# A Flamingo block on one Trainium2 core: the key weights' high parts shared between ScalarE and VectorE on the way to the loop

## The chip, the cores and the metric

The kernel is one program on one core of a Trainium2 chip. The metric is the time of one execution on the device, in microseconds (us), and less is better. The engines are TensorE (PE; PEld is its weight load), VectorE (DVE), ScalarE (ACT), GpSimd (POOL) and SyncE (SP), which issues the loads and stores. Each engine works through its own queue in order, and semaphores tie the queues together.

## What is computed

Eight batches of 224 tokens attend to 750 context rows and to themselves, with a gated residual, and then go through a gated feed-forward layer of spiking neurons. The part that matters here is the layer norm of the inputs and the keys and values made of them:

```python
def layernorm(x, g, b):
    mu = jnp.mean(x, axis=-1, keepdims=True)
    var = jnp.var(x, axis=-1, keepdims=True)
    return (x - mu) * jax.lax.rsqrt(var + EPS) * g + b
xn = layernorm(x, gm, bm)              # x: the 750 context rows of a batch, 512 wide
ln = layernorm(latents, gl, bl)        # latents: its 224 tokens, normalised once before
q = ln @ Wq
kv = jnp.concatenate([xn, ln], axis=-2) @ Wkv
k, v = jnp.split(kv, 2, axis=-1)
q, k, v = (heads(q), heads(k), heads(v))
q = q / scale
sim = jnp.einsum('bhid,bhjd->bhij', q, k)
attn = jax.nn.softmax(sim - stop_gradient(max(sim)), axis=-1)
out = jnp.einsum('bhij,bhjd->bhid', attn, v)
x = x + jnp.tanh(g_xattn[0]) * (out @ Wout)
# then h = square(relu(layernorm(x) @ W_fc.T)), y = h @ W_proj.T, five threshold steps, x + tanh(g_ffn) * spikes / 5
```

## The kernel before

**Numbers in two parts.** Every product with a weight is made of two-part numbers: a high part in the format fp32r (part 0) and the rest, value minus high part (part 1). A product is three passes: high by high, rest of the weight by high, high by rest of the data. For a weight `w` of 512 x 512 there are four pieces (k = 0 to 3, 128 rows each). `split_hi` (ACT, L1339) writes a piece's high part from the staged load, and `split_lo` writes its rest: on DVE at L1801, on POOL at L2099. `w_hi` counts the high parts, `w_lo[i]` the rests of weight i, where i is 0 for the keys (`wk`), 1 for the queries (`wq`), 2 for the values (`wv`), 3 for the output (`wo`).

**Tiles.** The 974 rows of a batch (750 of context, 224 tokens) lie in eight tiles: 0 to 3 of 128 rows, 4 and 5 of 119, 6 and 7 of 112. For the first batch, DVE makes mean and variance of two tiles at a time (`first_statistics`, L1593 to L1604), POOL the scale factors (`first_root_of`, L2036 and L2088). The scaling of tiles 0, 2, 5, 7 is on ACT (`first_norm`, L1349), that of 1, 3, 4, 6 on POOL (L2093). PE transposes the scaled tiles (`first_transposes`, L813): tiles 0 to 3 give the first 512 columns, tiles 4 to 7 the other 462. ACT writes the high part of each of four transposed chunks into `xT` (`hi_chunks`, L1142), DVE the rest (`lo_chunks`, L1614). Two columns at each end of `xT` hold offset vectors; ACT (L1365) and DVE (L1820) write them.

**The way to the loop.** Ahead of the loop over the batches, all queues are written out by hand, in one fixed order each. PE's is: six warming transposes, tiles 0 to 3, the first key products (`first_keys_hi`), tiles 4 to 7, the passes with the rest of `xT` (`first_keys_lo`), the second keys, queries, first scores, first values. `first_keys_hi` takes piece k as soon as its high part and chunk k are there, then waits for all four rests (`w_lo[0]`) and does the passes with them. The four transposes of tile 4 overwrite the bank from which the rest of chunk k is read, so each waits for that rest (`xlo_done`).

SP loads in this order: tiles 0 and 1, tiles 2 and 3, the key weights in two halves (`wk_in[0]` for pieces 0 and 1, `wk_in[1]` for 2 and 3), tiles 4 and 5, tiles 6 and 7, the query weights, and, once the key rests are there, the value weights.

On DVE, behind the statistics of tiles 0 to 3, stand the rests of pieces 0 and 1, the end columns, one small difference (`dshift`, L1821), the statistics of tiles 4 to 7, then the rests of the four chunks. On POOL, behind tiles 1 and 3, stand the rests of pieces 2 and 3, then the factors and the scaling of tiles 4 and 6.

Of the kernel before, what the change touches and what calls it, by code (L numbers as in the profile page):

```python
# [20 lines left out]
def flamingo_block(nc, x, ctx_in, g_xattn, g_ffn, Wq, Wkv, Wout, gm, bm, gl, bl, WfcT, WprojT, out):  # L21
# [5 lines left out]
    DC = D // P  # L27
# [43 lines left out]
    with keep:  # L71
        def sb(stack, name, shape, dt=F32):
            return stack.enter_context(nc.sbuf_tensor(name, shape, dt))

        def sem(name):
            return keep.enter_context(nc.semaphore(name))
# [33 lines left out]
        wk = sb(a, "wk", [P, 2, DC, D], F32R)  # L110
# [91 lines left out]
        def kq_index(c, u, first):  # L202

            return FIRST.index((c, u)) if first else 3 * c + u
# [9 lines left out]
        def kq_bank(c, u, first):  # L214
# [2 lines left out]
                return (work[0], work[1], heads_out, work[0], work[1], heads_out, maxes, work[1])[FIRST.index((c, u))]  # L217
            return work[kq_index(c, u, first) % 2]

        def value_bank(t):  # L220
            return work[(t + t // VF) % 2]

# [21 lines left out]
        gate_half = sem("gate_half")  # L244
        w_in = [sem(f"w_in{i}") for i in range(4)]
        w_hi = sem("w_hi")
        w_lo = [sem(f"w_lo{i}") for i in range(4)]
        wk_in = [sem(f"wk_in{i}") for i in range(2)]
        pair_in = [sem(f"pair_in{i}") for i in range(TILES // 2)]
# [104 lines left out]
        staged = [vals[:, (i % 2) * DC:(i % 2 + 1) * DC, :] for i in range(4)]  # L354
# [140 lines left out]
        def _(pe):  # L495
# [53 lines left out]
            def values(b, t, after_out=False, first=False):  # L549

                if t < 2:
                    pe.wait_ge(kq_done, (4, 8)[t] if first else b * 12 + (7 + t))
                elif t < 6:
                    if after_out:
                        pe.wait_ge(x1_done[t - 4], b + 1)
                    pe.wait_ge(v_done, b * VF + (t - 1))
                elif t == 6:
                    pe.wait_ge(v_done, b * VF + 6)
                else:
                    pe.wait_ge(kq_done, b * 12 + 9)  # L560
                product(value_bank(t)[0:ROWS[t], :], lambda i, k: xT[:, i, k, XO + AT[t]:XO + AT[t] + ROWS[t]],
                        lambda i, k: wv[:, i, k, :], DC).then_inc(v_mm, 1)
# [260 lines left out]
            def first_product(c, w, a, k, u=0, start=False, stop=False):  # L823

                lo, hi = ((0, HALF), (XO + half_of(c, True), XO + KEYS))[u]
                return pe.matmul(kq_bank(c, u, True)[:, 0:hi - lo], wk[:, w, k, c * P:(c + 1) * P], xT[:, a, k, lo:hi],  # L826
                                 start=start, stop=stop)

            def first_keys_hi():

                pe.wait_ge(ends_hi, 2)
                for k in range(DC):
                    pe.wait_ge(w_hi, k + 1)
                    pe.wait_ge(xhi_done, k + 1)
                    for c in range(2):
                        first_product(c, 0, 0, k, start=(k == 0))
                pe.wait_ge(w_lo[0], DC)
                for c in range(2):
                    for k in range(DC):
                        first_product(c, 1, 0, k)  # L840
                for w in range(2):
                    for k in range(DC):
                        first_product(2, w, 0, k, start=(w == 0 and k == 0))
# [32 lines left out]
            warm(6)  # L876
            first_transposes(0, 1, 2, 3)
            first_keys_hi()
            first_transposes(4, 5, 6, 7)
            first_keys_lo()  # L880
# [176 lines left out]
        def _(act):  # L1057
# [76 lines left out]
            def hi_chunks(b, g, *ks):  # L1134

                for k in ks:
                    if g == 0 and k == 0:
                        act.wait_ge(kq_mm, b * 12)
                        act.wait_ge(v_mm, b * TILES)
                    act.wait_ge(tr_done, b * 2 * DC + (g * DC + k + 1))  # L1140
                    if g == 0:
                        act.activation(xT[:, 0, k, XO:XO + HALF], score[:, k, 0:HALF], ACT.Copy,  # L1142
                                       scale=gain[:, 0, k:k + 1]).then_inc(xhi_done, 1)
                    else:
                        act.activation(xT[:, 0, k, XO + HALF:XO + T], score[:, k, 0:2 * CT], ACT.Copy,
                                       scale=gain[:, 0, k:k + 1])
                        act.activation(xT[:, 0, k, XO + T:XO + KEYS], score[:, k, 2 * CT:2 * CT + L], ACT.Copy,
                                       scale=gain[:, 2, k:k + 1]).then_inc(xhi_done, 1)
# [184 lines left out]
            def split_hi(i, w, *ks):  # L1333
                for k in ks:
                    if i == 0:
                        act.wait_ge(wk_in[k // 2], 16)
                    else:
                        act.wait_ge(w_in[i], 16)
                    act.activation(w[:, 0, k, :], staged[i][:, k, :], ACT.Copy,  # L1339
                                   scale=QSCALE if i == 1 else 1.0).then_inc(w_hi, 1)  # L1340
# [5 lines left out]
            def first_norm(t):  # L1346
                r = ROWS[t]
                act.wait_ge(first_rstd, t // 2 + 1)
                act.activation(xin[0:r, t, :], xin[0:r, t, :], ACT.Identity, bias=nmr[0:r, t:t + 1],  # L1349
                               scale=rstd[0:r, t:t + 1]).then_inc(ln_act, 1)  # L1350
# [5 lines left out]
            act.wait_ge(const_ready, 4)  # L1356
            act.activation(gate[:, 0:1], halfneg[:, 0:1], ACT.Copy)
            first_norm(0)
            split_hi(0, wk, 0, 1)
            act.wait_ge(vec_mm, 1)  # L1360
            act.activation(gain[:, :, :], heads_out[:, 0:4 * DC].rearrange("p (v k) -> p v k", v=4),
                           ACT.Copy).then_inc(gain_ready, 1)
            act.wait_ge(gain_ready, 1)
            for end in ENDS:
                act.activation(xT[:, 0, :, end], end_columns, ACT.Copy).then_inc(ends_hi, 1)  # L1365
            act.activation(offsets[:, 0, :, LT:P], bm_columns, ACT.Copy).then_inc(shift_hi, 1)
            first_norm(2)
            split_hi(0, wk, 2, 3)
            hi_chunks(0, 0, 0, 1, 2, 3)
            first_norm(5)  # L1370
            first_norm(7)
            split_hi(1, wq, 0, 1, 2)
# [95 lines left out]
        def _(dve):  # L1468
# [117 lines left out]
            def first_statistics(i):  # L1586

                ts = (2 * i, 2 * i + 1)
                dve.wait_ge(pair_in[i], 16)
                if i == 2:  # L1590
                    dve.wait_ge(ends_in, 16)
                for t in ts:
                    dve.bn_stats(bn[0:ROWS[t], t, :], xin[0:ROWS[t], t, :]).then_inc(bn_done, 1)  # L1593
                dve.wait_ge(bn_done, ts[-1] + 1)
                dve.tensor_copy(tick[:, 0:1], halfneg[:, 0:1])
                for t in ts:
                    dve.bn_aggr(mv[0:ROWS[t], t, :], bn[0:ROWS[t], t, :]).then_inc(mv_done, 1)
                two = slice(2 * i, 2 * i + 2)
                dve.wait_ge(mv_done, ts[-1] + 1)
                dve.tensor_scalar(nmu[:, two], mv[:, two, 0], -1.0, None, ALU.mult)  # L1600
                if i < 3:
                    dve.tensor_scalar(ve[:, two], mv[:, two, 1], EPS, None, ALU.add).then_inc(first_ve, 1)
                else:
                    dve.tensor_scalar(ve[:, two], mv[:, two, 1], 1.0 + EPS, EPS * EPS, ALU.mult,  # L1604
                                      ALU.add).then_inc(first_ve, 1)
# [191 lines left out]

            def split_lo(i, w, *ks):
                for k in ks:
                    dve.wait_ge(w_hi, i * DC + (k + 1))  # L1800
                    dve.scalar_tensor_tensor(w[:, 1, k, :], staged[i][:, k, :], QSCALE if i == 1 else 1.0,  # L1801
                                             w[:, 0, k, :].bitcast(F32), ALU.mult, ALU.subtract).then_inc(w_lo[i], 1)

# [9 lines left out]
                dve.tensor_copy(tick[:, 1 + i:2 + i], halfneg[:, 0:1]).then_inc(x1_done[i], 1)  # L1813
            first_statistics(0)
            first_statistics(1)
            split_lo(0, wk, 0, 1)
            dve.wait_ge(gain_ready, 1)
            for i, end in enumerate(ENDS):
                dve.wait_ge(ends_hi, i + 1)
                dve.tensor_tensor(xT[:, 1, :, end], end_columns, xT[:, 0, :, end].bitcast(F32), ALU.subtract)  # L1820
            dve.tensor_tensor(dshift[:, :], gain[:, 3, :], gain[:, 1, :], ALU.subtract).then_inc(dshift_done, 1)  # L1821
            first_statistics(2)
            first_statistics(3)
            lo_chunks(0, 0)
# [195 lines left out]
        def _(pool):  # L2020
# [69 lines left out]
            def first_norm(t):  # L2090
                r = ROWS[t]
                pool.wait_ge(first_rstd, t // 2 + 1)
                pool.tensor_scalar(xin[0:r, t, :], xin[0:r, t, :], rstd[0:r, t:t + 1], nmr[0:r, t:t + 1],  # L2093
                                   ALU.mult, ALU.add).then_inc(ln_pool, 1)

            def split_lo(i, w, *ks):
                for k in ks:
                    pool.wait_ge(w_hi, i * DC + (k + 1))
                    pool.tensor_tensor(w[:, 1, k, :], staged[i][:, k, :], w[:, 0, k, :].bitcast(F32),  # L2099
                                       ALU.subtract).then_inc(w_lo[i], 1)  # L2100

# [51 lines left out]
```

## Time and profile before

| | us |
|---|---|
| median of 3 runs | 1043.2 |
| lowest and highest of them | 1042.61, 1043.29 |
| the profiled execution | 1042.75 |
| its span, first to last instruction | 1040.9 |
| PE busy | 1024.1 (98% of the span) |
| DVE busy | 781.9 (75%) |
| ACT busy | 592.0 (57%) |
| POOL busy | 311.2 (30%) |

The span is what the trace shows; the time of an execution is a little longer, since it holds what lies around the first and the last instruction. Busy shares are means over the whole program. The stretch that the change touches is the first 20 us or so, and it is read from timelines of that stretch.

### The profile page before, as it was taken

To read this page: it belongs to the slowest core of one execution; us is meant where nothing else is said; L and a number is where in the kernel's file an instruction comes from. 1 tells how busy PE (TensorE), PEld (TensorE's weight loads), DVE (VectorE), ACT (ScalarE), POOL (GpSimd) and SP (SyncE) were. 2 spreads that over 40 slices of the span, in tenths; PEclk is the share of its full clock that TensorE was granted. 3 is DMA by queue.
4 is the path that set the end of the run, shared out by engine and by line. 5 is a ranking of instruction groups with operands and counts; after the bars stand their busy time and mean duration, and the time that the engine had idled before them with its cause. 6 is when DMAs were issued, how large, how long until landed. Compare 5 with 4: busy or idle time off the path is not lost.

```text
span 1040.9 us, 18764 instructions
## 1 busy us (share of the span) xinstructions
PE 1024.1 (98%) x6919; PEld 840.9 (81%) x6919; DVE 781.9 (75%) x1228; ACT 592.0 (57%) x1147; POOL 311.2 (30%) x289
## 2 busy tenths in 40 slices
PE   6999999999999999999999999999999999999997
PEld 5878778878878877887887887777888888998887
DVE  7589978887896897888789687879433654584766
ACT  6667476566457647656645764566455433455535
POOL 5444443444336344344433634343000000000000
PEclk9999999999999999999999999999999999999999
DMA  6402001100300400110030020132430001201011
GB/s 199 136 2 78 2 1 56 58 1 10 102 0 0 112 0 0 60 52 0 10 102 0 0 76 0 36 94 60 149 122 21 1 1 41 82 1 41 21 61 42
DMA packets 32232, 47.54 MB, mean 46 GB/s; under 512 B 2617, under 2 KB 11849, under 8 KB 32185
## 3 DMA queue, kind: packets, MB, share of 16 engines
q1 hardware_dynamic: 32132, 46.87, 14.5%
q8 instruction: 30, 0.49, 0.2%
q14 instruction: 17, 0.14, 0.0%
q10 hardware_dynamic: 53, 0.04, 0.0%
HBM read 39.56 MB, written 7.34 MB: 45 GB/s over the span
## 4 chain that ended last, share of the span: by engine, by line
PE 94%; DVE 4%; DMA 1%; issue 1%; ACT 0%; SPq 0%; DVEq 0%
PE work L501 40%; PE work L660 14%; PE score L673 13%; PE heads_out L610 9%; PE score L584 9%; PE score L516 2%; PE heads_out L622 1%; PE score L929 1%; PE work L826 1%; DVE top L1479 1%; DMA vals<-in_L_xattn_Wkv 1%; DVE on L1563 1%; PE maxes L597 1%; DVE probs L1515 1%; PE heads_out L501 0%
## 5 line engine op out<-in xcount | busy, mean ns | idle before, releaser
L2031 POOL TENSOR_TENSOR dsum<-dsum,probs 128x448 f32<-128x448 f32 (+1 forms) x186 | 219.9, 1182 | 14.6
L501 PE MATMUL work<-wv,xT 128*128 128x512 f32 (+2 forms) x768 | 187.1, 398 | 0.4 <-DVE kst L1528 0.4
L501 PE MATMUL work<-xT,wk 128*128 128x512 f32 (+2 forms) x708 | 167.5, 388 | 0.0
L501 PEld LDWEIGHTS work<-wv,xT 128*128 128x128 f32 (+2 forms) x768 | 137.6, 183 | 37.0 <-issue 2.3
L660 PE MATMUL work<-zT,wf 128*128 128x512 f32 (+1 forms) x768 | 164.1, 364 | 0.0
L1067 ACT ACTIVATE probs<-score 128x448 f32<-128x448 f32 (+2 forms) x256 | 119.2, 548 | 76.9 <-PE score L584 76.9
L660 PEld LDWEIGHTS work<-zT,wf 128*128 128x128 f32 x768 | 131.5, 189 | 23.0 <-issue 0.7
L501 PEld LDWEIGHTS work<-xT,wk 128*128 128x128 f32 x708 | 129.7, 188 | 24.4 <-DVE qst L1533 0.4
L1515 DVE TENSOR_TENSOR probs<-probs,maxes 128x1792 f32<-128x1792 f32 x64 | 128.4, 2017 | 1.1
L2028 POOL TENSOR_TENSOR dsum<-probs 128x448 f32<-128x448 f32 x31 | 35.7, 1150 | 277.9 <-ACT probs L1073 277.9
L673 PE MATMUL score<-hT,wp 128*128 128x512 f32 (+1 forms) x576 | 117.4, 354 | 0.0
L2036 POOL TENSOR_TENSOR rstd<-ve,halfneg 128x4 f32<-128x4 f32 (+1 forms) x22 | 25.0, 1134 | 284.9 <-ACT ve L1173 200.7
L673 PEld LDWEIGHTS score<-hT,wp 128*128 128x128 f32 x576 | 96.1, 189 | 14.9
L1190 ACT ACTIVATE relu<-work 128x512 f32<-128x512 f32 (+1 forms) x64 | 34.8, 543 | 123.5 <-PE work L660 123.3
L584 PEld LDWEIGHTS score<-qst,kst 64*128 64x128 f32 (+2 forms) x1536 | 87.6, 181 | 21.2 <-issue 21.0
L610 PE MATMUL heads_out<-probs,vals 128*64 128x224 f32 (+1 forms) x992 | 100.8, 356 | 0.0
L1072 ACT ACTIVATE probs<-probs 128x1344 f32<-128x1344 f32 x64 | 85.7, 1338 | 26.4 <-DVE probs L1515 26.4
L584 PE MATMUL score<-qst,kst 64*128 64x224 f32 (+2 forms) x1536 | 99.8, 275 | 0.0
L1654 DVE TENSOR_TENSOR hT<-h,hT 128x512 fp32r<-128x512 f32 (+1 forms) x48 | 29.1, 606 | 87.9 <-ACT hT L1202 87.6
L610 PEld LDWEIGHTS heads_out<-probs,vals 128*64 128x64 f32 (+1 forms) x992 | 68.4, 137 | 26.6 <-issue 5.6
L1479 DVE TENSOR_TENSOR top<-score,top 112x448 f32<-112x448 f32 (+1 forms) x128 | 72.1, 617 | 17.7 <-ACT probs L1067 17.4
L1528 DVE SCALAR_TENSOR_TENSOR kst<-work,shift,kst 128x224 fp32r<-128x224 f32 (+4 forms) x93 | 48.6, 551 | 25.7 <-ACT kst L1099 13.8
(218 smaller groups left out, 1428.0 us busy)
## 6 DMA issues: line engine op xcount, KB each, us to landing
xin<-in_ctx SPq DMA_DIRECT2D x28, 256.0 KB, 3.9
neuron<-in_L_ffn_W_fc SPq DMA_DIRECT2D x16, 256.0 KB, 3.1
neuron<-in_L_ffn_W_proj SPq DMA_DIRECT2D x16, 256.0 KB, 2.9
xin<-in_ctx SPq DMA_DIRECT2D x14, 238.0 KB
xin<-in_x SPq DMA_DIRECT2D x14, 224.0 KB, 7.0
zt<-x_scratch SPq DMA_DIRECT2D x3, 1024.0 KB, 5.7
fin<-x_scratch SPq DMA_DIRECT2D x3, 1024.0 KB, 5.6
out<-fin SPq DMA_DIRECT2D x10, 256.0 KB, 2.1
```

Of the source, the lines that this page charges most:

```text
L501: mm = pe.matmul(bank, lhs(i, k), rhs(j, k), start=(n == 0), stop=(n == len(passes) * chunks - 1))
L584: mm = pe.matmul(score[0:ROWS[t], 2 * (k % 2) + e, t % 2 * L:(t % 2 + 1) * L], kst[rows, s, i, AT[t]:AT[t] + ROWS[t]], qst[rows, s, j, :], ...
L610: mm = pe.matmul(bank[e * DH:(e + 1) * DH, 0:L], vals[0:ROWS[t], t, h * DH:(h + 1) * DH], probs[0:ROWS[t], h % 4, t * L:(t + 1) * L], star ...
L660: mm = pe.matmul(up_bank(j)[:, 0:n], wf[:, w, j, k * P:(k + 1) * P], zT[:, a_, k, 0:n], start=(m == 0 and k == 0), stop=(m == len(PASSES) ...
L673: mm = pe.matmul(score[:, d, 0:n], wp[:, w, j, d * P:(d + 1) * P], h_part(g, j, a_)[:, 0:n], start=(j == 0 and m == 0), stop=(j == FC - 1 ...
L1067: act.activation(probs[0:r, (2 * p + e) % 4, 2 * k * L:(2 * k + 2) * L], score[0:r, 2 * (k % 2) + e, 0:2 * L], ACT.Copy).then_inc(s_copied, 1)
L1072: act.activation(probs[:, h % 4, 0:CTX_TILES * L], probs[:, h % 4, 0:CTX_TILES * L], ACT.Exp)
L1479: dve.tensor_tensor(top[0:r, e, :], score[0:r, 2 * (k % 2) + e, 0:2 * L], other, ALU.max).then_inc(top_done, 1)
L1515: dve.tensor_tensor(v, v, row.to_broadcast([P, TILES, L]), ALU.subtract).then_inc(sub_done, 1)
L1528: ins = dve.scalar_tensor_tensor(kst[:, s, 1, lo:hi], bank[:, lo - at:hi - at], shift[:, 0, c, v:v + 1], kst[:, s, 0, lo:hi].bitcast(F32), ...
L2028: pool.tensor_tensor(total, tile(0), tile(1), ALU.add).then_inc(dchain, 1)
L2031: pool.tensor_tensor(total[0:ROWS[t]], total[0:ROWS[t]], tile(t), ALU.add).then_inc(dchain if t < TILES - 1 else dsum_done, 1)
```

## The change

The high parts of key pieces 2 and 3 are now made by DVE, by a plain copy from the staged load (L1825 in the new numbering), ahead of the end columns; the rests of pieces 0 and 1 move behind `dshift`. A new semaphore, `wk_hi_late`, counts these two copies, and `hi_ready` gives the semaphore and the count for a piece's high part. On ACT, tile 2 is scaled behind piece 0, piece 1 comes behind the end columns, and the offsets' small write comes behind the four chunks. POOL still makes the rests of pieces 2 and 3, and waits for the copies.

```diff
+        def hi_ready(i, k):
+            if i == 0:
+                return (w_hi, k + 1) if k < 2 else (wk_hi_late, k - 1)
+            return w_hi, 2 + (i - 1) * DC + (k + 1)
...
                 for k in range(DC):                      # PE, first_keys_hi
-                    pe.wait_ge(w_hi, k + 1)
+                    pe.wait_ge(*hi_ready(0, k))
                     pe.wait_ge(xhi_done, k + 1)
...
             first_norm(0)                                # ACT
-            split_hi(0, wk, 0, 1)
+            split_hi(0, wk, 0)
+            first_norm(2)
             act.wait_ge(vec_mm, 1)
...
             for end in ENDS:
                 act.activation(xT[:, 0, :, end], end_columns, ACT.Copy).then_inc(ends_hi, 1)
+            split_hi(0, wk, 1)
+            hi_chunks(0, 0, 0, 1, 2, 3)
             act.activation(offsets[:, 0, :, LT:P], bm_columns, ACT.Copy).then_inc(shift_hi, 1)
-            first_norm(2)
-            split_hi(0, wk, 2, 3)
-            hi_chunks(0, 0, 0, 1, 2, 3)
             first_norm(5)
...
             first_statistics(1)                          # DVE
-            split_lo(0, wk, 0, 1)
+            for k in range(2, DC):
+                dve.wait_ge(wk_in[1], 16)
+                dve.tensor_copy(wk[:, 0, k, :], staged[0][:, k, :]).then_inc(wk_hi_late, 1)
             dve.wait_ge(gain_ready, 1)
...
             dve.tensor_tensor(dshift[:, :], gain[:, 3, :], gain[:, 1, :], ALU.subtract).then_inc(dshift_done, 1)
+            split_lo(0, wk, 0, 1)
             first_statistics(2)
...
             def split_lo(i, w, *ks):                     # DVE and POOL
                 for k in ks:
-                    pool.wait_ge(w_hi, i * DC + (k + 1))
+                    pool.wait_ge(*hi_ready(i, k))
```

How the queues stand, first ACT's at the start: `xin` is a tile (L1349, L1356 in the new numbering: the scaling), `wk` a weight piece, `gain` the layer norm vectors, `xT` of 4x2 an end column pair, `xT` of 512 a chunk. Before:

```order
L1349 ACTIVATE xin<-xin,nmr,rstd 128x512
L1339 ACTIVATE wk<-vals 128x512 x2
L1361 ACTIVATE gain<-heads_out 128x16
L1365 ACTIVATE xT<-gain 128x4x2 x2
L1366 ACTIVATE offsets<-gain 128x4x16
L1349 ACTIVATE xin<-xin,nmr,rstd 128x512
L1339 ACTIVATE wk<-vals 128x512 x2
L1142 ACTIVATE xT<-score,gain 128x512 x4
```

ACT's queue at the same place now:

```order
L1356 ACTIVATE xin<-xin,nmr,rstd 128x512
L1346 ACTIVATE wk<-vals 128x512
L1356 ACTIVATE xin<-xin,nmr,rstd 128x512
L1369 ACTIVATE gain<-heads_out 128x16
L1373 ACTIVATE xT<-gain 128x4x2 x2
L1346 ACTIVATE wk<-vals 128x512
L1149 ACTIVATE xT<-score,gain 128x512 x4
L1376 ACTIVATE offsets<-gain 128x4x16
```

The second tile has moved up by six operations, two pieces have left the queue, and the offsets come behind the chunks. DVE's queue from the end of the statistics of tiles 2 and 3 to those of tiles 4 and 5 (`BN_STATS`), before:

```order
L1602 TENSOR_SCALAR ve<-mv 128x2
L1801 SCALAR_TENSOR_TENSOR wk<-vals,wk 128x512 x2
L1820 TENSOR_TENSOR xT<-gain,xT 128x4x2 x2
L1821 TENSOR_TENSOR dshift<-gain 128x4
L1593 BN_STATS bn<-xin 119x6 x2
```

DVE's queue at the same place now:

```order
L1609 TENSOR_SCALAR ve<-mv 128x2
L1825 CAST wk<-vals 128x512 x2
L1829 TENSOR_TENSOR xT<-gain,xT 128x4x2 x2
L1830 TENSOR_TENSOR dshift<-gain 128x4
L1808 SCALAR_TENSOR_TENSOR wk<-vals,wk 128x512 x2
L1600 BN_STATS bn<-xin 119x6 x2
```

Two copies have come in ahead of the end columns, and the two rests stand between `dshift` and the next statistics. The rows of POOL and PE are the same as before, but for what they wait for.

## Rows read from the trace of the kernel before

**Rows 1.** The page: the span, and PE's busy time.

```profile
span 1040.9 us, 18764 instructions
...
PE 1024.1 (98%) x6919; PEld 840.9 (81%) x6919; DVE 781.9 (75%) x1228; ACT 592.0 (57%) x1147; POOL 311.2 (30%) x289
```

**Rows 2.** Chain of waits, 0 to 50 us: start us, us, what.

```profile
1.74 7.09 DMA vals<-in_L_xattn_Wkv
...
13.04 4.28 PE work L826 x16
...
36.32 0.99 ACT probs L1067 x2
```

**Rows 3.** Timeline, ACT: start us, us, engine, line, operation, count, [idle before <-releaser].

```profile
8.85 1.15 ACT L1339 ACTIVATE wk<-vals 128x512 fp32r<-128x512 f32 x2 [0.55 <-DMA vals<-in_L_xattn_Wkv]
...
10.10 0.31 ACT L1365 ACTIVATE xT<-gain 128x8 fp32r<-128x8 f32 x2
...
10.46 0.80 ACT L1349 ACTIVATE xin<-xin,nmr,rstd 128x512 f32<-128x512 f32 x1
...
11.17 1.14 ACT L1339 ACTIVATE wk<-vals 128x512 fp32r<-128x512 f32 x2
...
12.21 2.42 ACT L1142 ACTIVATE xT<-score,gain 128x512 fp32r<-128x512 f32 x4
```

**Rows 4.** Timeline, PE: transposes L813, products L826 (15.31 is the ninth).

```profile
9.18 1.78 PE L813 MATMUL score<-ident,xin 128*128 128x128 f32 x8
...
11.32 1.10 PE L813 MATMUL score<-ident,xin 128*128 128x128 f32 x8 [0.35 <-ACT xin L1349]
13.04 4.28 PE L826 MATMUL work<-xT,wk 128*128 128x512 f32 x16 [0.63 <-ACT xT L1142]
...
15.31 0.40 PE L826 MATMUL work<-xT,wk 128*128 128x512 f32 x1
...
18.98 1.75 PE L813 MATMUL score<-ident,xin 119*128 119x119 f32 x16
```

**Rows 5.** Timeline, DVE; last, line L1820 alone: ns min/median/max, first and last start.

```profile
7.84 0.51 DVE L1600 TENSOR_SCALAR nmu<-mv 128x2 f32<-128x2 f32 x1
...
9.52 1.29 DVE L1801 SCALAR_TENSOR_TENSOR wk<-vals,wk 128x512 fp32r<-128x512 f32 x2 [1.11 <-ACT wk L1339]
...
10.73 0.66 DVE L1820 TENSOR_TENSOR xT<-gain,xT 128x8 fp32r<-128x8 f32 x2
...
12.49 1.29 DVE L1593 BATCH_NORM_STATS2 bn<-xin 119x6 f32<-119x512 f32 x2 [1.03 <-DMA xin<-in_ctx]
...
16.19 2.72 DVE L1614 SCALAR_TENSOR_TENSOR xT<-score,gain,xT 128x512 fp32r<-128x512 f32 x4
...
L1820 DVE TENSOR_TENSOR xT<-gain,xT x2: 159/369/579, 10.7 to 10.8; 128x8 fp32r<-128x8 f32 x2
```

**Rows 6.** Timeline, POOL: scaling L2093, rests L2099.

```profile
7.55 0.77 POOL L2093 TENSOR_SCALAR xin<-xin,rstd,nmr 128x512 f32<-128x512 f32 x1
...
9.57 1.80 POOL L2093 TENSOR_SCALAR xin<-xin,rstd,nmr 128x512 f32<-128x512 f32 x1
...
11.87 2.52 POOL L2099 TENSOR_TENSOR wk<-vals,wk 128x512 fp32r<-128x512 f32 x2 [0.50 <-ACT wk L1339]
...
17.32 1.53 POOL L2093 TENSOR_SCALAR xin<-xin,rstd,nmr 119x512 f32<-119x512 f32 x2
```

**Rows 7.** SP's issue of the two key weight halves, and their time to landing.

```profile
1.74 0.98 SPq L411 DMA_DIRECT2D vals<-in_L_xattn_Wkv  x2
...
DMA to landing us min/median/max: 7.1/7.7/8.4
```

**Rows 8.** Timeline near 40 us, DVE and POOL; then L1487 over the program.

```profile
40.12 1.20 DVE L1487 TENSOR_TENSOR top<-top 128x448 f32<-128x448 f32 x1
...
40.80 1.68 POOL L2099 TENSOR_TENSOR wo<-vals,wo 128x512 fp32r<-128x512 f32 x1
...
L1487 DVE TENSOR_TENSOR top<-top x32: 611/626/1497, 40.1 to 706.0; 128x448 f32<-128x448 f32 x32
```

More of the change, by code:

```diff
@@ L246, in flamingo_block @@
         w_hi = sem("w_hi")
+        wk_hi_late = sem("wk_hi_late")
         w_lo = [sem(f"w_lo{i}") for i in range(4)]
@@ L1799, in split_lo @@
                 for k in ks:
-                    dve.wait_ge(w_hi, i * DC + (k + 1))
+                    dve.wait_ge(*hi_ready(i, k))
                     dve.scalar_tensor_tensor(w[:, 1, k, :], staged[i][:, k, :], QSCALE if i == 1 else 1.0,
```

## The prediction

> **What bounds the kernel now.** I read the page first: TensorE (PE) is busy 1024.1 us of a span of 1040.9 [rows 1]. What it isn't busy lies mostly at the start, so the chain of waits over the first 50 us comes next [rows 2]. There the loads, ScalarE (ACT) and the tile scaling lead to the first key products at 13.04 us, and from there the chain stays on PE until 36 us. The change lies between 8.8 and about 19 us, so I then laid the timelines of the four engines side by side [rows 3 to 6]. Behind 19 us nothing is moved, and PE is released there by work that itself waits for PE. I therefore take a delay of PE at about 19 us to go one to one into the end. The profiled execution took 1042.75 us against a span of 1040.9, 1.85 us lying around the span; the median of the three runs is 1043.2, 0.45 us above that. A shift worked out in this trace is added to the median.
>
> **What the start waits for.** ACT sets the first chunk of xT: its queue runs without a gap from 8.85 us (two key pieces, gain, end columns, offsets, tile 2, two key pieces) to chunk 0 at 12.21 [rows 3]. The transposes of tile 2 start only at 11.32, behind its scaling at 10.46 to 11.26, after the first eight had ended at 10.96 [rows 3, 4]. The four chunks then come every 0.58 us, and PE follows them until the ninth product, the first with a rest of the weights, at 15.31 [rows 4]. That product needs all four rests. GpSimd (POOL) ended the last of them at 14.39 [rows 6], a slack of 0.9 us. Later PE transposes tiles 4 to 7 from 18.98 [rows 4]. Tile 4's four transposes each need the rest of an xT chunk; the four rests run on VectorE (DVE) from 16.19 to 18.91 [rows 5]. The fourth transpose starts near 18.98 + 3 x 0.11 = 19.31 (16 in 1.75 us, 0.11 each), so the slack on DVE is only 19.31 - 18.91 less a hand-over of 0.05, or 0.35 us.
>
> **Part 1, ACT and tile 2: a gain at the first chunk.** ACT does piece 0 (8.85 to about 9.45, half of two in 1.15 us), then tile 2. Its scale factors are ready when POOL starts tile 3's scaling at 9.57, on the same factors [rows 3, 6]. So tile 2 runs from about 9.5 to 10.3, gain and end columns end near 10.75, piece 1 near 11.3; two pieces of 0.57 us are gone from ACT and one small write moves behind the chunks, where ACT has time. Tile 3's scaling on POOL took 1.80 us where tile 1's took 0.77; it now runs beside an idle DVE, say 0.77 us, to 10.34 [rows 6]. PE then goes straight on from tile 1 at 10.90. Its first eight transposes took 0.22 us each and the second eight 0.14 [rows 4]; at the first rate the fifth of the new eight ends at 12.1, at the later 0.11 near 11.6. I take 11.75, between them. Chunk 0 moves from 12.21 to 11.75: 0.46 us (0.1 to 0.6). Carried on alone, the ninth product would be due at 14.85.
>
> **Part 2, the copies on DVE.** DVE is free from 8.40, but the second half of the key weights, issued at 1.74 + 0.98 - 0.47 = 2.25, lands 8.4 us later, at 10.65 [rows 7]. The copies wait for it, and behind them in DVE's queue stand the end columns, dshift, the two moved rests, and the statistics of tiles 4 to 7. No row has a 128x512 copy by DVE; the two-input rest of that size took 0.69 us (two in 1.29), a 128x8 operation 0.16, so two copies are 0.3 to 1.3 us. I take 0.8: 10.67 to 11.45. The Trainium skill (VectorE: DVE Perf Modes, the perf-mode tier table) gives fp32 copies in SBUF twice the rate of a two-input operation; by its terms one would be an estimated 0.42 us, and the pair some 0.8. PE needs pieces 2 and 3 only at about 13.7 and 14.3, so that the copies themselves are covered on PE.
>
> Without any interference DVE then does the end columns and dshift (0.3) and two rests (1.29) by 12.86, and the next statistics start at 12.8 where they started at 12.49 on their load [rows 5]: 0.3 us late, just inside the slack of 0.35.
>
> **Part 3, DVE and POOL side by side.** Before, DVE's rests ended at 10.81 and POOL's rests ran 11.87 to 14.39 beside statistics, undisturbed (1.26 us each) [rows 5, 6]. Now POOL's two rests become ready at 11.1 and 11.5, and DVE's two at 11.6: they meet. Rows show what a meeting costs. Tile 3's scaling stood 1.03 us longer beside DVE's two rests (9.52 to 10.81). A 128x8 end column took 0.58 instead of 0.16 and ended at 11.38, when that scaling ended. A 128x2 scalar operation of DVE at 7.84 took 0.51, to the end of POOL's 0.77 [rows 5, 6]. At 40.12 an operation of 0.62 us took 1.20, until POOL's first rest had ended, and POOL's next took 1.68 [rows 8]. So here they take turns, whole instructions each. DVE kept its turn from one rest to the next, and POOL got in behind the tiny end column. The Trainium skill (SBUF — State Buffer, Who interferes with whom) says this as an exclusive lock, held by whoever starts first, for operations of DVE with two SBUF inputs or in a two-port mode. By that rule the trace agrees.
>
> In the order of the change POOL is ready when DVE reaches the tiny end columns, so as before I let POOL in there: POOL's first rest 11.45 to 12.55. Then the second end column, dshift and, without a gap, DVE's two rests 12.55 to 13.85; POOL's second rest follows, 13.8 to 14.87 (1.26 us less the 0.2 that it spends before it reads, as tile 3's 0.77 counted from 10.8 gives). Two results:
> - all rests ready at 14.9, and the ninth product at 14.95 to 15.0 in place of 15.31: 0.3 us early, most of part 1 kept.
> - DVE's statistics begin at 13.77 in place of 12.49: 1.28 us late. From there DVE has no gap up to the four xT rests, and tile 4's and 6's scaling on POOL (17.32 to 18.85) hangs on the same statistics. The xT rests end at 18.91 + 1.28 = 20.19, PE's fourth transpose goes at 20.25 in place of 19.31.
>
> The sum at 19 us is +1.28 - 0.35 = +0.93 us; the gain of part 1 is spent as waiting at tile 4. The weights of the values, whose load waits for the rests (14.4), come half a microsecond later and are wanted at 26.5: nothing.
>
> **Rivals.**
> 1. *DVE keeps its turn through all its queue.* For it: two rests in a row shut POOL out at 9.57. Then the statistics are 0.3 us late, inside the slack, but POOL's rests run 12.85 to 15.2, and the ninth product is at 15.3, as before. Sum 0 (-0.35 to +0.3): 1043.2. The part 1 gain goes into the wait for POOL. Even with no interference the sum isn't below -0.1, since DVE's 0.35 is spent.
> 2. *POOL gets in twice*, behind the end column and again behind dshift. For it: dshift is as short. Against it: POOL spends 0.2 us before its second reads, and DVE's first rest is queued. DVE's rests then run 13.66 to 14.95 and the statistics are 2.4 us late: +2.4 - 0.35 = +2.05, or 1045.2. It decides if POOL's second rest reads before DVE's first; from a statistics delay of 2.44 us on, the total is slower by over 0.2%.
> 3. *The gain arrives.* If the second half of the key weights landed 0.5 us or more earlier than in this trace, DVE would meet an idle POOL and the slack would hold: at best -0.35 us, 1042.85. Against it: 8.4 us to landing, and nothing ahead of it in the queue changes.
> 4. *PE slows down.* It now stands still for about 1 us between 18.9 and 20.3. Its first transposes ran at half the later rate after a long idle [rows 4]; if that came back for some fifteen products of 0.23 us each, it would be +3 us more, 1047. Against it: the gap of 0.63 us before 13.04 left the rate alone [rows 4].
>
> **Chances and numbers.** My forecast (POOL in once) 0.5; rival 1 0.25; rival 2 0.17; rival 3 0.05; rival 4 0.03. Forecast 1043.2 + 0.93 = 1044.1. The range goes from 0.4 under the median of before, which holds rival 1 and nearly all of rival 3, up to 2.2 over it, for rival 2: 1042.8 to 1045.4. A measurement of this kernel can tell 0.2%, 2.1 us, from no change. Slower by more than that: half of rival 2 and rival 4, 0.11. Faster by more: no path here is that long, 0.02 for what I don't see. Within 0.2%: 0.87.
>
> **What would show it.** In the changed trace: tile 3's scaling near 0.77 us; tile 2's transposes at once behind tile 1's; chunk 0 at 11.6 to 11.9; DVE's copies from 10.65; an end column of about 1.1 us that ends with POOL's first rest; POOL's second rest at some 2.3 us beside DVE's two; the statistics of tile 4 at 13.8; PE idle around tile 4's transposes; and tiles 4 to 7 done some 0.9 us later than before. It is wrong if the statistics begin before 13 us (rival 1 or 3), or after 14.5 (rival 2), or if a wait later on swallows the shift.

## The result

The changed kernel takes 1045.68 us (median of 13 runs, 1044.37 to 1046.82), the kernel before 1043.2; the ratio is 1.0023 with a 95% interval of 1.0015 to 1.003. One of the 13 runs of the kernel before took 5788.16 us and is left out of the comparison; the other twelve lie between 1042.5 and 1043.38. The changed kernel is slower by some 2.5 us, more than the 1044.1 that was forecast and 0.3 us outside the range. The profiled execution took 1045.42 us with a span of 1043.5, 2.6 us over the span of before [rows 1].

The page of the changed kernel, span and busy times. PE has the same 6919 instructions and is busy 1.0 us longer than before; 0.7 us of this lie in its first sixteen transposes (3.62 us for 2.88). Otherwise PE merely starts the rest of its work later:

```profile
span 1043.5 us, 18764 instructions
...
PE 1025.1 (98%) x6919; PEld 841.3 (81%) x6919; DVE 784.1 (75%) x1230; ACT 591.4 (57%) x1145; POOL 309.9 (30%) x289
```

The chain of waits of the changed kernel over the first 50 us (start us, us, what). Before, it went over to PE at 13.04 and stayed there until 36 us [rows 2]. Now it runs through the load and DVE up to 22 us:

```profile
2.25 9.23 DMA vals<-in_L_xattn_Wkv
...
12.27 1.22 DVE xT L1829 x2
13.49 1.17 DVE dshift L1830
14.67 1.20 DVE wk L1808 x2
15.87 1.21 DVE bn L1600 x2
...
19.48 2.64 DVE xT L1621 x4
...
22.16 1.50 PE score L820 x13
```

DVE's timeline of the changed kernel answers to [rows 5]. The columns are start us, us, engine, line, operation, count and the idle time ahead with its releaser:

```profile
11.51 0.76 DVE L1825 CAST wk<-vals 128x512 fp32r<-128x512 f32 x2 [2.81 <-DMA vals<-in_L_xattn_Wkv]
12.18 1.31 DVE L1829 TENSOR_TENSOR xT<-gain,xT 128x8 fp32r<-128x8 f32 x2
13.41 1.25 DVE L1830 TENSOR_TENSOR dshift<-gain 128x4 f32<-128x4 f32 x1
14.59 1.28 DVE L1808 SCALAR_TENSOR_TENSOR wk<-vals,wk 128x512 fp32r<-128x512 f32 x2
15.79 1.27 DVE L1600 BATCH_NORM_STATS2 bn<-xin 119x6 f32<-119x512 f32 x2
```

POOL's timeline answers to [rows 6]. Its two rests of the key weights are the two things that DVE's small operations wait for:

```profile
9.86 0.77 POOL L2103 TENSOR_SCALAR xin<-xin,rstd,nmr 128x512 f32<-128x512 f32 x1
12.02 2.63 POOL L2109 TENSOR_TENSOR wk<-vals,wk 128x512 fp32r<-128x512 f32 x2 [1.38 <-DVE wk L1825]
```

PE's timeline answers to [rows 4]:

```profile
9.72 3.62 PE L820 MATMUL score<-ident,xin 128*128 128x128 f32 x16
13.66 4.38 PE L833 MATMUL work<-xT,wk 128*128 128x512 f32 x16 [0.32 <-ACT xT L1149]
...
21.34 0.53 PE L820 MATMUL score<-ident,xin 119*128 119x119 f32 x3 [1.49 <-POOL xin L2103]
22.16 1.50 PE L820 MATMUL score<-ident,xin 119*128 119x119 f32 x13 [0.29 <-DVE xT L1621]
```

The first end column (8 columns) and `dshift` (4 columns) take 1.2 us each, until one of POOL's rests ends (12.02 to 13.40, 13.35 to 14.65). The statistics of tile 4 begin at 15.79 instead of 12.49, 3.30 us late. PE stands still from 19.85 to 21.34, and its fourth transpose of tile 4 goes at 22.16 instead of about 19.31. From there nearly the whole shift is kept. The first transpose of the row maxima, before and now:

```profile
46.34 0.27 PE L592 MATMUL maxes<-ident,rmax 128*14 128x128 f32 x1
...
49.29 0.27 PE L599 MATMUL maxes<-ident,rmax 128*14 128x128 f32 x1
```

That is +2.95. The one at 344.28 is at 347.10 (+2.82), one at 708.04 is at 710.71 (+2.67), and the execution is longer by 2.67 us (1045.42 for 1042.75): 0.28 us of the shift are lost on the way.

### The profile page after: what moved, and what is told of

Read it like the earlier page. It is cut to its first block, busy times and chain, and to the rows that moved or that the text cites. A ratio compares the mean times of both kernels' runs of the same rounds, so it can differ in the third digit from the quotient of the medians.

```text
span 1043.5 us, 18764 instructions
## 1 busy us (share of the span) xinstructions
PE 1025.1 (98%) x6919; PEld 841.3 (81%) x6919; DVE 784.1 (75%) x1230; ACT 591.4 (57%) x1145; POOL 309.9 (30%) x289
## 4 chain that ended last, share of the span: by engine, by line
PE 93%; DVE 5%; DMA 1%; issue 1%; ACT 0%; SPq 0%; DVEq 0%
PE work L508 40%; PE work L667 14%; PE score L680 13%; PE heads_out L617 9%; PE score L591 8%; PE score L523 2%; PE heads_out L629 1%; PE score L936 1%; DMA vals<-in_L_xattn_Wkv 1%; DVE top L1486 1%; DVE on L1570 1%; PE maxes L604 1%; DVE probs L1522 1%; PE heads_out L508 0%; PE work L833 0%
```

## The experiments

Three numbers are read from every trace. The *statistics' delay* is the start of tile 4's statistics less 12.49. The *shift* is the start of PE's first transpose of the row maxima less 46.34, the value of the kernel before. The *landing* is when the second half of the key weights is there. The *theory of turns* in the expectations says that DVE and POOL, where they meet, work in turns of whole instructions. All ratios are to the kernel before on the same chip.

### The kernel before, once more

> The kernel before once more, for a second trace. It shows how far the loads' landing and the rate of PE's first transposes move from one execution to the next without any edit. If the second half of the key weights lands between 10.6 and 11.6 us here too, the time stays at 1043.2 +- 0.4, since ACT wants it only at 11.2 to 11.7. If the late landing (11.48 in the changed kernel against 10.65) came of the change, it is at 10.65 +- 0.1 here.

One execution, 1043.6 us. The second half of the key weights was there at 2.25 + 8.2 = 10.4 us (the longer of two landings, 6.5 and 8.2 us), earlier than either value expected, so the landing moves by itself. PE's rows in this trace of the unchanged kernel:

```profile
9.90 3.62 PE L813 MATMUL score<-ident,xin 128*128 128x128 f32 x16
13.84 4.27 PE L826 MATMUL work<-xT,wk 128*128 128x512 f32 x16 [0.32 <-ACT xT L1142]
```

All sixteen transposes took 0.22 us each here, where the trace that the prediction was made from had the second eight at 0.14 [rows 4]. ACT was done with its weights at 11.75 and waited 1.26 us for PE, its first chunk coming at 13.01. So what sets the first chunk is ACT in one execution and PE's slow transposes in another. PE's first work hangs on the small vectors' load, 7.66 us in one trace and 8.39 in the other, but that alone doesn't settle the rate: in the kernel with POOL's rests behind DVE's, further down, PE began at 6.67 us and its sixteen transposes took 3.62 us again. What sets it stays open. The later first chunk is paid for to the end here: the first product is 0.80 us late, the first transpose of the row maxima is at 47.12 (+0.78), and the execution took 0.85 us more than the one that the prediction was read from. DVE's slack in this trace is larger by about as much.

### The changed kernel, twice more

> The changed kernel once more, for a second trace and times on the chip of the others. Theory of turns: the statistics of tile 4 start at the landing of the second half plus 4.3 us (copies 0.8, two small operations 2.4 that each end with one of POOL's rests, two rests 1.2), and the total moves with the landing: +2.0 for a landing at 10.7, +2.9 for 11.5. Theory of the landing alone: the start follows the landing at 2.5 us or less, and a trace with an early landing shows no loss.

> The changed kernel again, beside the next one. Theory of the clock: PE stands still for 1.2 to 1.5 us ahead of tile 4's transposes, and in part of the executions the granted clock is then halved for some 3 us, which adds about 1.5 to 2 us; so the times fall into a lower group near 1044.5 and an upper one near 1046.3. Rival, the spread comes of the landing alone: the times are spread evenly over 2 us.

On one chip 1044.86 us (ratio 1.0016, interval 1.0007 to 1.0025), on another 1044.46 (1.002, 1.0011 to 1.0029). Both medians, +1.67 and +1.41 us, lie inside the range that was forecast. The landing was earlier in both traces, 10.43 and 10.3, and DVE met POOL twice again. The second trace, DVE:

```profile
11.33 1.31 DVE L1829 TENSOR_TENSOR xT<-gain,xT 128x8 fp32r<-128x8 f32 x2
12.57 1.24 DVE L1830 TENSOR_TENSOR dshift<-gain 128x4 f32<-128x4 f32 x1
13.73 1.28 DVE L1808 SCALAR_TENSOR_TENSOR wk<-vals,wk 128x512 fp32r<-128x512 f32 x2
14.93 1.27 DVE L1600 BATCH_NORM_STATS2 bn<-xin 119x6 f32<-119x512 f32 x2
```

| trace of the changed kernel | landing | statistics' delay | delay less 0.35 | shift measured |
|---|---|---|---|---|
| first | 11.5 | 3.30 | 2.95 | 2.95 |
| second | 10.4 | 2.44 | 2.09 | 2.09 |
| third | 10.3 | 2.09 | 1.74 | 1.74 |

The statistics begin 4.3 to 4.5 us behind the landing in all three, as the theory of turns says, and an early landing doesn't save the kernel. In the second trace the copies met POOL too: the first took 0.63 us for 0.43, until tile 3's scaling ended at 10.80, which makes 4.5 us out of 4.3. The slack of 0.35 us, that of the trace of before, gives the shift to the hundredth, since behind the statistics everything up to the row maxima takes the same time.

### POOL's two rests cut to 8 columns

```diff
+            pool.memset(wk[:, 1, 2:DC, :].bitcast(F32), 0.0)
...
-                    pool.tensor_tensor(w[:, 1, k, :], staged[i][:, k, :], w[:, 0, k, :].bitcast(F32),
+                    n = 8 if i == 0 else D
+                    pool.tensor_tensor(w[:, 1, k, 0:n], staged[i][:, k, 0:n], w[:, 0, k, 0:n].bitcast(F32),
                                        ALU.subtract).then_inc(w_lo[i], 1)
```

> The changed kernel with POOL's rests of key pieces 2 and 3 cut from 512 to 8 columns (the remainder is zero and filled early), so that DVE meets nobody; the rest of the program is unchanged. Theory of turns: the small operations of DVE take 0.15 each, the statistics of tile 4 start 2.3 us behind the landing, total 0 to +1. Theory of queue length (DVE simply has 0.8 us of copies and 1.3 us of rests more in front of the statistics): nothing changes by this edit, total +2.5.

1042.83 us, ratio 0.9996 (0.9987 to 1.0005). The loss is gone. This kernel leaves out all but 8 columns of those two rests. DVE, POOL and PE in its trace:

```profile
11.08 0.23 DVE L1829 TENSOR_TENSOR xT<-gain,xT 128x8 fp32r<-128x8 f32 x2
11.24 0.15 DVE L1830 TENSOR_TENSOR dshift<-gain 128x4 f32<-128x4 f32 x1
11.31 1.29 DVE L1808 SCALAR_TENSOR_TENSOR wk<-vals,wk 128x512 fp32r<-128x512 f32 x2
12.53 1.27 DVE L1600 BATCH_NORM_STATS2 bn<-xin 119x6 f32<-119x512 f32 x2
...
10.91 0.55 POOL L2111 TENSOR_TENSOR wk<-vals,wk 128x8 fp32r<-128x8 f32 x2 [0.36 <-DVE wk L1825]
...
12.30 4.25 PE L833 MATMUL work<-xT,wk 128*128 128x512 f32 x16 [0.63 <-ACT xT L1149]
...
18.91 1.50 PE L820 MATMUL score<-ident,xin 119*128 119x119 f32 x13 [0.23 <-DVE xT L1621]
```

The same queue of DVE takes its own time, 0.23 and 0.15 us for the small operations, and the statistics start at 12.53. So it is not the length of DVE's queue that costs, but the meeting with POOL. PE's products even begin at 12.30 for 13.04. How much of that is tile 2's place can't be told, since PE's first work began at 6.86 us in this trace and at 7.66 in that of before. At tile 4 PE waits 0.23 us for DVE, and the shift is only -0.28. DVE's slack is used up, as the prediction had it for an undisturbed change, though its floor for that was -0.1 (-0.35 with an early landing); the landing here was 10.35.

### DVE's small operations ahead of the copies

```diff
             first_statistics(1)
-            for k in range(2, DC):                        # the two copies
-                ...
             dve.wait_ge(gain_ready, 1)
             for i, end in enumerate(ENDS):
...
             dve.tensor_tensor(dshift[:, :], gain[:, 3, :], gain[:, 1, :], ALU.subtract).then_inc(dshift_done, 1)
+            for k in range(2, DC):                        # the two copies
+                ...
             split_lo(0, wk, 0, 1)
```

> The changed kernel with the end columns and dshift on DVE ahead of the copies, where they meet nothing of POOL. Theory of turns: POOL gets in only behind a small operation of DVE, so now DVE keeps its turn from the copies through its two rests (0.76 + 1.28), the statistics of tile 4 start about 2.1 us behind the landing instead of 4.3, POOL's rests run after that and end 4.6 us behind the landing; total 0 to +0.9 against the kernel before. Rival, each rest of POOL gets in whatever DVE's operation is: the two meetings remain, the statistics are still 4.2 us behind the landing, and the total stays at +2 to +3.

1045.39 us, ratio 1.0021 (1.0012 to 1.003): the theory as it stood, that POOL gets in only behind a small operation, falls, and the rival's total of +2 to +3 holds. DVE and POOL, one row an instruction:

```profile
12.08 1.75 DVE L1808 SCALAR_TENSOR_TENSOR wk<-vals,wk 128x512 fp32r<-128x512 f32 x1
13.76 1.77 DVE L1808 SCALAR_TENSOR_TENSOR wk<-vals,wk 128x512 fp32r<-128x512 f32 x1
...
11.92 1.37 POOL L2109 TENSOR_TENSOR wk<-vals,wk 128x512 fp32r<-128x512 f32 x1 [1.13 <-DVE wk L1830]
13.25 1.74 POOL L2109 TENSOR_TENSOR wk<-vals,wk 128x512 fp32r<-128x512 f32 x1
```

POOL's first rest starts at 11.92, during DVE's second copy, and runs to 13.29. DVE's first rest (0.68 us by itself) takes 1.75, to 13.83. POOL's second takes 1.74, to 14.99. DVE's second takes 1.77, to 15.53. They alternate here, one instruction each, large operations of DVE like small ones, and each rest of DVE ends 0.54 us behind POOL's. The prediction had read a preference for DVE out of one place [rows 5, 6]. The Trainium skill (SBUF — State Buffer, Who interferes with whom) has it that the order of issue decides, not the shape of the operation. By that rule the trace agrees, in that DVE's 128x512 rests wait here as its 128x8 and 128x4 operations did in the changed kernel.

The statistics came 5.4 us behind the landing, 10.05 in this trace, where the rival had 4.2. The end columns could start only at 11.18, when ACT's part of them was done, and the copies stood behind them until 11.41.

This trace also shows the second part of the loss. PE by stretches of 1 us (busy us and count, granted clock, DMA share, GB/s), and its timeline:

```profile
21.00:22.00 1.00, 0.69 (x5) 1.00 0.00 0
22.00:23.00 1.00, 1.00 (x8) 0.61 0.00 0
23.00:24.00 1.00, 1.00 (x8) 0.50 0.00 0
24.00:25.00 1.00, 1.00 (x5) 0.50 0.00 0
25.00:26.00 1.00, 1.00 (x5) 0.68 0.00 0
...
21.84 2.42 PE L820 MATMUL score<-ident,xin 119*128 119x119 f32 x13 [0.30 <-DVE xT L1621]
23.93 2.88 PE L833 MATMUL work<-xT,wk 128*128 128x512 f32 x8
```

PE had stood still for 1.45 us (19.56 to 21.01) and for 0.30 more. The granted clock then was 0.50 (1.2 GHz) from about 22.2 to 25.6. Thirteen transposes took 2.42 us where the other traces have 1.50, eight products 2.88 where they have 2.06, 1.7 us in all. The sum: 2.97 (statistics at 15.46) - 0.35 + 1.7 = 4.3, and the shift is 4.23.

### PE kept busy where it stood still

```diff
             first_keys_hi()
+            pe.wait_ge(gain_ready, 1)
+            for i in range(10):
+                pe.transpose(heads_out[:, i % DC * P:(i % DC + 1) * P], ident[:, :], ident[:, :])
             first_transposes(4, 5, 6, 7)
```

> The changed kernel with ten more transposes of the identity on PE (1.1 us, into a bank that is free) ahead of tile 4's transposes, where PE stood still. They do not help the chain: tile 4 still waits for its scaling. Theory of the clock: the granted clock stays at 1.00 and the upper group of times goes: all between 1043.9 and 1045.2, median 0.3 to 1 us under the changed kernel's of the same chip. Rival, the spread comes of the landing or the port: the same spread, and a median equal to or above the changed kernel's.

1044.79 us, ratio 1.0017 (1.0008 to 1.0026), beside 1044.46 of the changed kernel on that chip: the median isn't better, which misses the expectation. The spread shrank and the upper group is gone, but three of the 11 runs lie above the 1045.2 that was the bound. The times of the changed kernel lie in two groups: over its three sets of runs 23 of 35 lie at 1045.7 us or below, down to 1044.25, and 12 lie above, 1045.86 to 1046.82. On this chip they were 7 from 1044.25 to 1044.53 and 4 from 1045.86 to 1046.78. With the ten transposes all 11 lie between 1043.95 and 1045.65. In the first set the six runs above 1046 had a mean granted clock of 0.996 to 0.998, the others 0.998 or 0.999. All this fits an upper group in which the clock was halved behind the stand-still, as traced above in the small-operations kernel. It is argued and not shown, since no trace of an upper run of the changed kernel is there, the clocks of the groups overlap at 0.998 (one run at 1045.86 has 0.999), and in two of the three sets no wide gap parts the groups.

The trace of this kernel also says why its median isn't lower. The landing was 10.35, and tile 3's scaling ran until 11.00: the first copy took 0.86 us for 0.43. The delay is 2.65 and the shift 2.30, again 0.35 apart. For how many of the 11 runs this holds isn't known.

### The parts of the change, one at a time

ACT's part alone (tile 2 behind piece 0, pieces 1 to 3 behind the end columns, offsets behind the chunks):

```diff
             first_norm(0)
-            split_hi(0, wk, 0, 1)
+            split_hi(0, wk, 0)
+            first_norm(2)
...
-            act.activation(offsets[:, 0, :, LT:P], bm_columns, ACT.Copy).then_inc(shift_hi, 1)
-            first_norm(2)
-            split_hi(0, wk, 2, 3)
+            split_hi(0, wk, 1, 2, 3)
             hi_chunks(0, 0, 0, 1, 2, 3)
+            act.activation(offsets[:, 0, :, LT:P], bm_columns, ACT.Copy).then_inc(shift_hi, 1)
```

> The kernel before with ACT's part of the change alone: tile 2 behind piece 0, then the vectors and end columns, then pieces 1 to 3, the chunks and the offsets' write. DVE and POOL keep their queues and their rests. Piece 1 is now ready at about 11.3 us instead of 10.0, and DVE's rest of it stands ahead of its small operations. Theory of turns: that rest and the small operations meet POOL's two rests (ready at about 11.9 and 12.4), and the statistics of tile 4 start at 13.5 to 14.5 us instead of 12.5; total +0.7 to +1.7. Rival, ACT's order is harmless and the copies do it: total -0.3 to +0.2.

1044.57 us, ratio 1.0012 (1.0003 to 1.0021), within the total that the theory of turns gave; the statistics start at 14.88, later than its 13.5 to 14.5. DVE's rest of piece 1 stands ahead of the small operations and can't start before 11.84. Behind it they meet both of POOL's rests:

```profile
11.84 0.69 DVE L1801 SCALAR_TENSOR_TENSOR wk<-vals,wk 128x512 fp32r<-128x512 f32 x1 [1.86 <-ACT wk L1339]
12.45 1.33 DVE L1820 TENSOR_TENSOR xT<-gain,xT 128x8 fp32r<-128x8 f32 x2
13.71 1.25 DVE L1821 TENSOR_TENSOR dshift<-gain 128x4 f32<-128x4 f32 x1
14.88 1.27 DVE L1593 BATCH_NORM_STATS2 bn<-xin 119x6 f32<-119x512 f32 x2
```

Delay 2.39, shift 2.03, with no copy on DVE at all. The median is 1.4 us over that of before, about as much as the lower group of the whole change. PE stood still for only 0.52 us ahead of tile 4, and no run lies above 1044.78.

DVE's moved rests alone:

```diff
             first_statistics(1)
-            split_lo(0, wk, 0, 1)
             dve.wait_ge(gain_ready, 1)
...
             dve.tensor_tensor(dshift[:, :], gain[:, 3, :], gain[:, 1, :], ALU.subtract).then_inc(dshift_done, 1)
+            split_lo(0, wk, 0, 1)
```

> The kernel before with DVE's rests of pieces 0 and 1 moved behind dshift, and nothing else. Theory of turns: DVE is through with them at 11.9 us, before POOL's rests begin at 11.9, and nobody meets; the statistics still start at their load, 12.5; total -0.1 to +0.2. Rival, the moved rests by themselves delay the statistics by their 1.3 us: total +0.9.

1043.36 us, ratio 1.0 (0.9991 to 1.0009). The rests are through at 12.41, later than expected, and the statistics start behind them, at 12.33. They did meet POOL: its first rest started at 11.90 and took 1.64 us for 1.27. The trace's shift is 0.52, but its first product was late by as much (13.57). Moving the rests costs nothing that the median shows.

The copies alone (`split_lo(0, wk, 0, 1)`, then the two copies, then the end columns; ACT in its old order without pieces 2 and 3):

> The kernel before with the two copies on DVE (behind its rests of pieces 0 and 1, ahead of the end columns), ACT in its old order less those two pieces. Theory of turns: an end column and dshift meet POOL's rests, the statistics start 3.2 us behind the landing of the second half (13.8 for a landing at 10.6); total +0.9 to +1.8, and the moved rests account for the remainder of the whole change. Rival, the copies alone cost what they take, 0.8 us, within the time in which DVE waits for its load: total -0.3 to +0.2.

1043.57 us, ratio 1.0004 (0.9995 to 1.0013). The +0.4 us lie between the theory's +0.9 to +1.8 and the rival's -0.3 to +0.2, and the interval reaches into both. The landing was not what held the copies here (DVE began them at 10.50, straight behind its rests), and only one of the two meetings was long:

```profile
11.17 0.65 DVE L1829 TENSOR_TENSOR xT<-gain,xT 128x8 fp32r<-128x8 f32 x2
11.75 1.24 DVE L1830 TENSOR_TENSOR dshift<-gain 128x4 f32<-128x4 f32 x1
12.91 1.27 DVE L1599 BATCH_NORM_STATS2 bn<-xin 119x6 f32<-119x512 f32 x2
...
10.14 1.59 POOL L2102 TENSOR_SCALAR xin<-xin,rstd,nmr 128x512 f32<-128x512 f32 x1
11.70 2.51 POOL L2108 TENSOR_TENSOR wk<-vals,wk 128x512 fp32r<-128x512 f32 x2
```

An end column waited for the end of tile 3's scaling (11.73) and dshift for POOL's first rest (12.95); the second rest ran beside the statistics and met nobody. The delay is 0.42 us, 0.07 more than the slack; the shift of 0.41 comes of PE's first product, 0.40 us late in this trace. The scaling of tile 3 took 1.59 us for 0.77: it started at 10.14, and both copies of DVE (10.50 to 11.26) went past it. That isn't one instruction each. (That they went past is read from these lengths.)

### The changed kernel with POOL's rests behind DVE's

```diff
             first_norm(3)
+            pool.wait_ge(w_lo[0], 2)
             split_lo(0, wk, 2, 3)
```

> The changed kernel, but POOL starts its rests of pieces 2 and 3 only when DVE's two rests are done. Theory of turns: every operation of DVE takes its own time, the statistics start 2.2 us behind the landing (12.6 to 13.7), POOL's rests end 4.7 us behind it (15.1 to 16.2), which PE wants at 14.6 to 15.9; total -0.3 to +0.6, some 2 us better than the change as it is. Rival, the loss is in the time that POOL's rests come: later rests make it worse, total over +2.5.

1043.66 us, ratio 1.0004 (0.9995 to 1.0013): one added wait takes back most of the loss, with all of the work still done. The statistics start at 13.23, 2.1 us behind the landing at 11.1. POOL's rests come so late that PE waits for them:

```profile
13.23 2.44 PE L833 MATMUL work<-xT,wk 128*128 128x512 f32 x8 [0.63 <-ACT xT L1149]
15.98 2.12 PE L833 MATMUL work<-xT,wk 128*128 128x512 f32 x8 [0.32 <-POOL wk L2109]
```

That wait isn't what is left of the loss. The trace's shift is 1.33 us, and at tile 4 PE waits for DVE again. The delay of 0.74 less 0.35 gives 0.39 of it; another 0.9 us comes of a meeting behind the statistics, where a 128x2 operation of DVE (L1607) took 1.07 us for 0.17, beside POOL's second rest.

None of the kernels is faster than the one before beyond its interval.

## Why the prediction was wrong, point by point

**Where it is decided: right.** Nothing behind 19 us was moved, the fourth transpose of tile 4 is where the change is paid, the slack there is 0.35 us in the trace that I read, and what is over it goes one to one into PE's work up to the row maxima at 46 us. Three traces of the changed kernel, that with the ten transposes, and that of ACT's part alone (2.39 - 0.35 = 2.04, measured 2.03) give it to 0.01 us. Up to the end 0.28 us of 2.95 are lost in the first trace.

**Part 1: the first chunk, mis-sized and mostly of the wrong sign.** I took 11.75 us. In the seven traces with this order of ACT it was 12.83, 12.38, 12.92, 12.60, 12.39, 11.91 and 11.47, and 13.01 in the second trace of the kernel before. The step that failed was the rate of PE's transposes: I took a mean of two rates seen in one trace, and the slow one can last through all sixteen, in the kernel before as well. Only the last two show a gain (first products at 12.75 and 12.30 for 13.04). Tile 3's scaling at 0.77 us in place of 1.80 was right, and brought nothing. (In ACT's queue tile 2 moved up by five operations, not six.)

**Part 2: the copies, right in size** (0.76 us for 0.8). They took 0.96 and 1.19 in two traces in which tile 3's scaling was still running. The bare durations add up to 13.04, not to the 12.86 given; the next statistics at 12.8 are right even so, since each start overlaps the end ahead by some 0.08 us: without POOL's rests they come 2.16 us behind the copies' start. Their landing was taken as a fixed 10.65; it lay between 10.3 and 11.5 in the changed kernel's traces. Before, ACT wanted that load only at 11.17, so the kernel hardly felt it. The copies put it ahead of all that DVE has left, where every tenth counts. In the first trace this is 0.8 us of the 3.30.

**Part 3: the turns, the step that decided.** "I let POOL in there: POOL's first rest 11.45 to 12.55. Then the second end column, dshift and, without a gap, DVE's two rests" is the sentence that fell. POOL got in twice. It was written down as rival 2 with a delay of 2.4 us and a shift of 2.05, at a chance of 0.17; the second trace has 2.44 and 2.09. I had given DVE a preference on the ground of one row, tile 3's scaling held through two of DVE's rests, against the rows of 40 us, where the two engines alternate [rows 8]. The experiment with the small operations first shows them alternate here too. Without POOL's rests the loss is gone, and with them put behind DVE's it falls from some 1.3 to 3.2 us to 0.5.

**Rival 4: called too unlikely.** The clock was halved behind PE's stand-still in one trace, that of the small operations first, at a cost of 1.7 us; in the changed kernel itself the upper group of 12 in 35 executions, some 1.9 us over the lower, is put down to it without a trace. I had it at 0.03 and +3 us, on a gap of 0.63 us that left the rate alone; the gap was 1.49, 1.19 and 0.29 us in the three traces of the changed kernel, none of which shows a halved clock. Six of the upper runs fell in the 13 of the first set, whose median lies at the upper end of the lower group. It is by this share that the first set's median left the range; those of the other two sets, 1044.86 and 1044.46, lie inside it. That is luck either way, since two meetings show in all three traces.

**The sum.** Lower group +1.3 us against the median of before, upper group +3.2. The forecast of +0.93 lies under both. One more step failed, and it hid part of the error: a shift read in one trace was added to the median of before. Once DVE sets the pace, a slow start of PE, as in the second trace of before, no longer counts, while the median of before has it in part (inferred from the two traces of that kernel). Added to the profiled execution, 1042.75, the three shifts give 1045.70, 1044.84 and 1044.49 for the measured 1045.42, 1044.93 and 1044.34; added to the median they give 0.45 more each.

What stays open: why in the kernel before POOL's scaling of tile 3, started at 9.57, let two operations of DVE pass instead of one, and why from 10.14, in the kernel with the copies alone, it let both copies pass behind the rest that was running. POOL's two-input rests never waited for more than one operation in these traces.

## What to carry to other kernels

Before work is moved onto VectorE, lay its queue beside GpSimd's. Where both work on SBUF at one time, count a meeting for each instruction, at the price of up to the other engine's whole instruction, even if one's own has 4 columns. Not every operation of VectorE meets: the statistics (BATCH_NORM_STATS2, 0.68 us each) kept their time beside GpSimd's rests. A change in ScalarE's order alone can bring such meetings about: here it cost about as much as the whole change in its lower group. Work that waits for a load, put ahead of everything else in a queue, takes on all of that load's spread, 1.2 us here. A slack found in one trace must be set against how far the loads and PE's first rate move from one execution to the next, and a second trace of the unchanged kernel shows that.

## What the runs showed of the hardware

- VectorE and GpSimd alternated by whole instructions wherever VectorE met GpSimd's two-input rests; twice a GpSimd scaling (one input) waited for more than one operation of VectorE (1.80 and 1.59 us for 0.77). A 128x4 operation of DVE took 1.25 us beside a rest of POOL and 0.15 without it. A 128x2 scalar operation of DVE with a single input took 1.07 us for 0.17 beside such a rest, in the kernel with POOL's rests behind DVE's:

```profile
14.89 1.07 DVE L1607 TENSOR_SCALAR nmu<-mv 128x2 f32<-128x2 f32 x1
```

- A 128x512 copy from fp32 to fp32r by DVE takes 0.42 us, against 0.68 for the two-input operation of the same size.
- A stand-still of PE of 1.45 us was followed by a granted clock of 0.50 for 3.4 us, beginning 1.2 us after PE was at work again. In the first trace of the changed kernel one of 1.49 us wasn't, so it isn't the length of the gap alone.
- The same load landed between 10.3 and 11.5 us after the start over three executions of the same program, with an unchanged queue.
